# Routing tiles 20 to 25 one at a time instead of in pairs, in a fused involution and mixture-of-experts kernel

## The chip, the core and the metric

The kernel runs on one core of a Trainium2 chip. The metric is the device time of one execution in microseconds (us). PE is the matrix engine (TensorE), DVE the vector engine, ACT the scalar engine, POOL is GpSimd, and SP issues most of the plain DMAs. Each engine works through its own list of instructions in order; semaphores tie the lists together.

## What is computed

```python
# x: (4, 128, 56, 56) float32
def _L0_conv_ref(x, reduce_w, reduce_b, span_w, span_b):      # K=7, G=16 groups
    patches = conv_general_dilated_patches(x, (7, 7), ...)     # 49 shifted copies
    h = einsum('bchw,oc->bohw', x, reduce_w) + reduce_b        # 128 -> 32 channels
    kern = einsum('bchw,oc->bohw', h, span_w) + span_b         # 32 -> 49*16
    return (kern * patches).sum(axis=3)                        # a kernel per pixel
def _L0_ffn_ref(x, router_w, w1, w2, w3):                      # 8 experts, top 2, hidden 341
    probs = softmax(flat @ router_w.T)
    topk_probs, topk_idx = top_k(probs, 2)
    topk_probs = topk_probs / (sum(topk_probs) + 1e-09)
    h = silu(flat @ w1[e].T) * (flat @ w3[e].T)                # for every expert
    out = einsum('ne,nec->nc', gates, h @ w2[e].T)
x = x + _L0_conv_ref(_ln_c(x), ...)
t = _to_tokens(x)
t = t + _L0_ffn_ref(_ln_t(t), ...)
```

There are 4 x 56 x 56 = 12,544 tokens of 128 channels, and each goes to two of the eight experts.

## The kernel before

**Tiles and steps.** The image is cut into 28 tiles of 8 rows (448 tokens, handled as 4 groups of 112). All engines' lists are written out from one clock of steps `S`. Tile t has the steps 25t to 25t+24: in each step PE makes the per-pixel kernels of two taps (L635, into `kern_ps`), and DVE multiplies them with the shifted image (L901, or L895 with L898; the last, single tap is L889). The products are summed by POOL (L1144, L1148, into `acc_p`) and by PE (L650, into `acc_ps`). The convolution ends with step 699 (`CONV_END` = 700). DVE's L1106 adds the input and gives `x1` of tile t in step 5 of the next tile; then ACT computes the statistics, POOL takes the inverse root (L1134, L1136: `rsqrt`), ACT normalises (L807) and makes a second copy (the `twin`), PE transposes (L601) and computes the logits (L606).

**Routing.** Tiles are routed in groups (`GROUPS_OF`): the pairs (0,1) to (24,25), then 26 and 27 alone. One routing takes 41 DVE instructions: 19 of `route` (L924 to L970: the two best experts and their gates), 4 of `place` (L982 to L995: each row's place in the expert's list), 18 of `table` (L1013 to L1055: which blocks of 512 rows are full now). They are small, at most 128 elements a partition, and stand between DVE's products at fixed steps after `ROUTER_AT`, the start of the tile behind the group: `route` at offsets 19 to 31, `place` at 27 to 29, `table` at 33 to 41. ACT's two exponentials come at 24, its `gates` (L792) at 32, and PE's counting matmuls (`rank`, L611 and L614) at 26. For groups routed inside the convolution the scratch operands lie in PSUM, in spare columns of `kern_ps`; for the last ones they lie in SBUF (`small_sb`, `wide_sb`). For a pair of tiles the instructions work on 8 groups of 112 tokens at once, for a single tile on 4.

**Scatters.** Behind its routing each tile's rows go to memory (`xs`) with 8 indirect DMAs of POOL (L1157), at the steps of `SCATTER_J`; the first scatter of a tile waits for that tile's places and gates. Scatters that find no step before 700 are put behind the first blocks' adds by `BEHIND`.

**Blocks.** 56 blocks of 512 rows go through the experts, in the order in which groups complete them. A block is 6 slots on PE (3 matmuls each: L672, L673, L676), with ACT's silu (L832) and DVE's product (`hid`, L1074); then PE multiplies with w2 (`third`, L583, into the one PSUM `bank`), ACT scales by the gate (`y_tok`, L737), and POOL adds the rows to the output with 4 indirect DMAs (L1169). The first add of a block waits until all adds of the block before have landed. In the convolution slots are dealt out 11 in 25 steps, and 192 of the 336 slots stand there; behind it they follow each other. A block may be loaded when its group's table is there and all scatters up to that group have landed. `READY[g]` is the step from which the lists assume that. Blocks 40 to 55 need the last tile's group.

**Behind step 700** POOL's list reads: four adds of block 31 (step 704), four scatters, `rsqrt` of tile 27 (step 709), adds of block 32 (step 710), three scatters, and so on to block 37: 22 scatters, 6 of tile 25 and 8 each of tiles 26 and 27. From block 38 on there are only adds.

Of the kernel before, what the change touches and what calls it, by code (L numbers as in the profile page):

```python
# [23 lines left out]
TILES = B * PER_IMG  # L24
# [23 lines left out]

GROUPS_OF = [(2 * i, 2 * i + 1) for i in range(13)] + [(26,), (27,)]
NG = len(GROUPS_OF)
GMAX = max(len(g) for g in GROUPS_OF) * SUBS
BT = 512
BSUBS = BT // 128
NBLOCKS = (2 * TOKENS - EXPERTS) // BT + EXPERTS
FULL = [max(0, -(-(2 * N * (g[-1] + 1) - EXPERTS * (BT - 1)) // BT)) for g in GROUPS_OF[:-1]] + [NBLOCKS]

# [27 lines left out]
def at(p, j):  # L86
    return p * TAPS + j
# [22 lines left out]
def off(g, what):  # L110
    if g == NG - 1:
        return LAST_OFF[what]
    return {"route": ROUTE_OFF, "rank": RANK_OFF, "exp": EXP_OFF, "place": PLACE_OFF, "gates": GATES_OFF, "table": TABLE_OFF}[what]

ROUTER_AT = [at(tiles[-1] + 1, 0) for tiles in GROUPS_OF]
SCATTER_AT = {}
READY = []
_free = FIRST  # L120
for _g, _tiles in enumerate(GROUPS_OF):
    _S = max(_free, ROUTER_AT[_g] + off(_g, "place")[-1] + 1)
# [154 lines left out]
def build(nc, x, w_red, b_red, w_span, router, w13, w2, ident, lower, consts, tabs, ids, empty, out):  # L277
    with ExitStack() as ctx:
# [153 lines left out]
        def group_of(t):  # L432
            return next(i for i, tiles in enumerate(GROUPS_OF) if t in tiles)

# [811 lines left out]
```

## Time and profile before

| | us |
|---|---|
| median of 3 runs (lowest, highest) | 1472.53 (1470.37, 1472.7) |
| the profiled execution | 1467.69 |
| its span, first to last instruction | 1465.9 |
| busy in it: PE, DVE, POOL, ACT | 1247.6, 1119.5, 1082.7, 582.1 |

The profiled execution is 4.8 us shorter than the median and lies below all three timed runs. Inside the span the product of the last tap of the last tile (L889) ends at 1179.7 us; what follows, 286 us, is the stage in which the other 24 blocks are computed.

### The profile page before, as it was taken

What the parts mean: (1) busy time and instruction counts of PE and PEld (TensorE: products, weight loads), DVE (VectorE), ACT (ScalarE), POOL (GpSimd) and SP (SyncE); (2) the same over time, 40 slices, a digit from 0 to 9 for tenths busy, and PEclk for the clock granted to TensorE, in tenths of its full rate; (3) what the DMA queues carried; (4) which work ended last, traced back from release to release, by engine and by line L of the source; (5) the groups of instructions that cost most, each with busy time, mean ns of one, the idle gap of its engine ahead of it and who ended that gap; (6) DMA issues with size and microseconds to landing.
All of it is one profiled execution on the core that took longest, in us unless ns stands there. A gap on an engine that the chain in (4) does not pass through costs nothing.

```text
span 1465.9 us, 23321 instructions
## 1 busy us (share of the span) xinstructions
PE 1247.6 (85%) x7763; PEld 1027.1 (70%) x7763; DVE 1119.5 (76%) x1663; ACT 582.1 (40%) x1961; POOL 1082.7 (74%) x781
## 2 busy tenths in 40 slices
PE   5898998978988989899898998899989877788781
PEld 3677777767867777777777777777777766676561
DVE  7999999998898988888889798888898954232220
ACT  5334333333443434534345353354434343333230
POOL 4767787765785878787788687867878867856565
PEclk9999999998999999999999999999999988899996
DMA  4111111121242322433224232343322446666652
GB/s 127 61 42 54 57 58 52 58 79 55 39 106 59 86 63 61 101 69 86 60 61 104 65 92 57 62 100 83 73 54 53 108 102 181 129 162 146 140 118 24
DMA packets 93347, 120.42 MB, mean 82 GB/s; under 512 B 11531, under 2 KB 72428, under 8 KB 93082
## 3 DMA queue, kind: packets, MB, share of 16 engines
q1 hardware_dynamic: 53802, 90.97, 20.6%
q0 software_dynamic: 39424, 27.96, 13.8%
q8 instruction: 62, 1.02, 0.3%
q14 instruction: 59, 0.48, 0.1%
HBM read 78.92 MB, written 42.65 MB: 83 GB/s over the span
## 4 chain that ended last, share of the span: by engine, by line
PE 43%; DVE 27%; issue 12%; POOL 10%; DMA 5%; ACT 3%; DVEq 0%; SPq 0%; POOLq 0%; ACTq 0%
PE acc_ps L650 14%; PE kern_ps L635 13%; DVE prod L901 12%; PE bank L583 7%; POOL out L1169 7%; DVE kern_ps L895 4%; DMA out<-y_tok,idx 4%; PE h_ps L672 2%; PE h_ps L673 2%; PE h_ps L676 2%; DVE hid L1074 2%; DVE prod L898 2%; POOL acc_p L1148 1%; DVE kern_ps L1047 1%; DVE xf_lo L1099 1%
## 5 line engine op out<-in xcount | busy, mean ns | idle before, releaser
L901 DVE TENSOR_TENSOR prod<-kern_ps,xn 128x896 f32<-128x896 f32 x592 | 627.0, 1082 | 49.6 <-PE kern_ps L635 47.2
L635 PE MATMUL kern_ps<-h_stack,span 98*128 98x448 f32 x1372 | 465.8, 424 | 107.8 <-DVE prod L901 66.2
L1148 POOL TENSOR_TENSOR acc_p<-acc_p,prod 128x896 f32<-128x896 f32 x180 | 414.3, 2302 | 77.5 <-DVE prod L901 74.1
L1169 POOL DMA_INDIRECT out<-y_tok,idx x224 | 351.4, 1569 | 136.0 <-issue 60.0
L650 PE MATMUL acc_ps<-ident_sb,prod 128*112 128x128 f32 x2960 | 394.9, 277 | 0.0
L650 PEld LDWEIGHTS acc_ps<-ident_sb,prod 128*112 128x112 f32 x2960 | 347.2, 135 | 38.1 <-DVE x L1106 7.5
L635 PEld LDWEIGHTS kern_ps<-h_stack,span 98*128 98x128 f32 x1372 | 224.4, 198 | 198.0 <-DVE prod L901 113.2
L1157 POOL DMA_INDIRECT xs<-rows_x,slots x224 | 219.0, 978 | 53.4 <-issue 32.1
L583 PEld LDWEIGHTS bank<-w2b,hid 114*128 114x128 f32 x1344 | 182.8, 203 | 47.0 <-DVE xf_lo L1099 21.1
L583 PE MATMUL bank<-w2b,hid 114*128 114x128 f32 x1344 | 190.8, 289 | 23.8 <-DVE xf_lo L1099 12.1
L832 ACT ACTIVATE silu<-h_ps 114x512 f32<-114x512 f32 x132 | 78.9, 598 | 243.7 <-PE h_ps L676 243.7
L1074 DVE TENSOR_TENSOR hid<-silu,h_ps 114x512 f32<-114x512 f32 x132 | 90.0, 682 | 91.3 <-ACT silu L832 44.0
L1144 POOL TENSOR_TENSOR acc_p<-prod 128x896 f32<-128x896 f32 x28 | 63.8, 2279 | 89.3 <-DVE prod L901 52.2
L672 PE MATMUL h_ps<-xf_hi,wb 128*114 128x512 f32 x264 | 119.4, 452 | 7.4 <-ACT silu L832 7.4
L737 ACT ACTIVATE y_tok<-bank,xb 128x128 f32<-128x128 f32 x224 | 64.1, 371 | 127.7 <-PE bank L583 115.3
L676 PE MATMUL h_ps<-xf_lo,wb 128*114 128x512 f32 x264 | 107.5, 407 | 0.0
L673 PE MATMUL h_ps<-xf_hi,wb 128*114 128x512 f32 x264 | 107.5, 407 | 0.0
L895 DVE TENSOR_TENSOR kern_ps<-kern_ps,xn 128x896 f32<-128x896 f32 x80 | 87.2, 1090 | 12.7 <-PE kern_ps L635 11.8
L898 DVE TENSOR_TENSOR prod<-kern_ps,prod 128x896 f32<-128x896 f32 x80 | 87.3, 1091 | 2.7
L1074 DVE TENSOR_TENSOR hid<-silu,kern_ps 114x512 f32<-114x512 f32 x36 | 24.7, 687 | 72.4 <-ACT silu L832 40.5
L1134 POOL TENSOR_TENSOR rstd_ln<-veps_ln,minus_half 112x4 f32<-112x4 f32 x56 | 66.3, 1184 | 15.4 <-ACT veps_ln L770 15.3
L807 ACT ACTIVATE rows_x<-x,shift_ln,rstd_ln 112x128 f32<-112x128 f32 x112 | 47.8, 486 | 43.0 <-POOL shift_ln L1136 43.0
(157 smaller groups left out, 1342.4 us busy)
## 6 DMA issues: line engine op xcount, KB each, us to landing
wb<-wexp SPq DMA_DIRECT2D x56, 684.0 KB, 4.8
xb<-xs SPq DMA_DIRECT2D x56, 264.0 KB, 3.3
w2b<-in_w SPq DMA_DIRECT2D x56, 171.0 KB
xt<-in_x SPq DMA_DIRECT2D x28, 224.0 KB, 3.4
out<-x SPq DMA_DIRECT2D x28, 224.0 KB, 2.7
wexp<-wb SPq DMA_DIRECT2D x8, 684.0 KB
xs<-rows_x,slots POOLq DMA_INDIRECT x224, 2.4
out<-y_tok,idx POOLq DMA_INDIRECT x224
```

Source lines behind the costliest of these rows:

```text
L583: i = mm(bank[:, k * C:(k + 1) * C], hid[:, (CPE * b + c) % HR, k * 128:(k + 1) * 128], w2b[:, b % 2, c, :], start=c == 0 and k == 0, stop ...
L635: last = mm(kern_ps[:, g % 2, i, 0:N], span[:, k * C:(k + 1) * C], h_stack[:, t % 2, :], start=True, stop=True)
L650: last = mm(acc_ps[0:SUB, k * C:(k + 1) * C], src[:, at_:at_ + SUB], ident_sb[:], is_transpose=True, start=u == BY_PE[t][0] and i == 0 and ...
L672: mm(ps, lo, xf_hi[:, b % 2, :], start=True, stop=False)
L673: mm(ps, hi, xf_hi[:, b % 2, :], start=False, stop=False)
L676: mm(ps, hi, xf_lo[:, b % 2, :], start=False, stop=True).then_inc(done, 1)
L895: v.tensor_tensor(kern.rearrange("p i (r w) -> p i r w", w=W), kern.rearrange("p i (r w) -> p i r w", w=W), taps, ALU.mult).then_inc(s_inn ...
L901: v.tensor_tensor(pair_rows(dst), kern.rearrange("p i (r w) -> p i r w", w=W), taps, ALU.mult).then_inc(s_prod, 1)
L1074: v.tensor_tensor(hid[:, n % HR, :], silu[:, n % 2, :], h_at(n, 1), ALU.mult).then_inc(s_hid, 1)
L1148: g_.tensor_tensor(acc_p[:], acc_p[:], prod[:, (t * TAPS + u) % PRING, :], ALU.add).then_inc(s_padd, 1)
L1157: g_.indirect_dma_start(out=xs, out_offset=bass.IndirectOffsetOnAxis(ap=slots[:, k, n:n + 1], axis=0), in_=rows_x[:, t % XN2RING, q, k, :] ...
L1169: g_.indirect_dma_start(out=out, out_offset=bass.IndirectOffsetOnAxis(ap=idx[:, b % XBRING, q:q + 1], axis=0), in_=y_tok[:, b % 2, q * C:( ...
```

## The change

The list of groups is altered: tiles 20 to 25 are no longer taken as (20,21), (22,23), (24,25), each of the six is a group of its own. Everything else follows from the tables that are computed from this list.

```diff
-GROUPS_OF = [(2 * i, 2 * i + 1) for i in range(13)] + [(26,), (27,)]
+GROUPS_OF = [(2 * i, 2 * i + 1) for i in range(10)] + [(t,) for t in range(20, TILES)]
```

So there are 18 groups instead of 15. The six tiles have routings of 41 DVE instructions each, where three routings served them before. 194 slots instead of 192 stand in the convolution, and 16 scatters instead of 22 behind it. The last group, tile 27, keeps its steps (718 to 721).

On DVE, inside tile 22, from the addition of the input (L1106, `x`) to the next `hid` product, the list had only products of the convolution:

```order
L1106 TENSOR_TENSOR x<-acc_ps,xt 112x512
L901 TENSOR_TENSOR prod<-kern_ps,xn 128x896 x4
L1074 TENSOR_TENSOR hid<-silu,h_ps 114x512
L901 TENSOR_TENSOR prod<-kern_ps,xn 128x896 x2
L895 TENSOR_TENSOR kern_ps<-kern_ps,xn 128x2x448
L898 TENSOR_TENSOR prod<-kern_ps,prod 128x896
```

In the changed kernel the same place reads:

```order
L1106 TENSOR_TENSOR x<-acc_ps,xt 112x512
L901 TENSOR_TENSOR prod<-kern_ps,xn 128x896
L964 TENSOR_SCALAR kern_ps<-kern_ps 112x4
L966 RECIPROCAL kern_ps<-kern_ps 112x4
L968 COPY gid<-kern_ps 112x4
L970 TENSOR_TENSOR gid<-kern_ps,e 112x4
L901 TENSOR_TENSOR prod<-kern_ps,xn 128x896 x2
L1013 COPY kern_ps<-base 1x8
L1015 SCALAR_TENSOR_TENSOR full<-kern_ps,thr 1x200
L1018 TENSOR_REDUCE kern_ps<-full 1x8
L901 TENSOR_TENSOR prod<-kern_ps,xn 128x896
L1074 TENSOR_TENSOR hid<-silu,h_ps 114x512
```

The end of `route` and the whole `table` of tile 20 have come between tile 22's products; tiles 24 and 26 get those of tiles 22 and 24 in the same way.

On POOL, from the last scatters inside the convolution, the list before is:

```order
L1157 DMA xs<-rows_x,slots 104960x132 x2
L1169 DMA out<-y_tok,idx 13056x128 x4
L1157 DMA xs<-rows_x,slots 104960x132 x4
L1134 TENSOR_TENSOR rstd_ln<-veps_ln,minus_half 112x4
L1136 TENSOR_TENSOR shift_ln<-negmean_ln,rstd_ln 112x4
L1169 DMA out<-y_tok,idx 13056x128 x4
L1157 DMA xs<-rows_x,slots 104960x132 x3
```

And now:

```order
L1157 DMA xs<-rows_x,slots 104960x132 x2
L1169 DMA out<-y_tok,idx 13056x128 x4
L1157 DMA xs<-rows_x,slots 104960x132 x4
L1169 DMA out<-y_tok,idx 13056x128 x4
L1157 DMA xs<-rows_x,slots 104960x132 x3
L1134 TENSOR_TENSOR rstd_ln<-veps_ln,minus_half 112x4
L1136 TENSOR_TENSOR shift_ln<-negmean_ln,rstd_ln 112x4
L1169 DMA out<-y_tok,idx 13056x128 x4
```

Block 31's adds stand at step 700 instead of 704, block 32's at 708 instead of 710, and so block 32's adds with the three scatters behind them have passed in front of tile 27's inverse root, which stays at step 709. The four scatters behind block 31 were tile 25's; now they are tile 26's, whose places and gates are written for steps 704 and 707.

## Rows read from the trace of the kernel before

**Rows 1.** Windows of tiles 17, 18, 21, 22, 25, 26: us, busy PE PEld DVE ACT POOL, clock

```profile
681.81:731.38 49.57, 44.38 (x276) 37.01 (x275) 43.20 (x71) 19.84 (x69) 36.63 (x27) 0.93 0.36 81
731.38:774.26 42.88, 39.83 (x261) 33.31 (x260) 36.90 (x47) 20.02 (x69) 37.42 (x28) 1.00 0.28 55
...
864.32:911.64 47.32, 42.88 (x272) 36.74 (x271) 42.39 (x70) 23.05 (x80) 36.00 (x27) 0.93 0.36 84
911.64:955.90 44.26, 39.39 (x241) 32.73 (x240) 37.50 (x49) 15.47 (x52) 39.34 (x29) 0.96 0.28 56
...
1045.63:1094.04 48.41, 43.44 (x276) 35.67 (x275) 43.21 (x71) 19.85 (x69) 36.56 (x27) 0.96 0.35 78
1094.04:1136.05 42.01, 39.59 (x261) 33.31 (x260) 36.90 (x47) 19.89 (x68) 36.25 (x27) 1.00 0.27 51
```

**Rows 2.** DVE groups by form: shapes xcount | busy us, mean ns

```profile
L1018 DVE TENSOR_REDUCE kern_ps<-full 1x8 f32<-1x200 f32 x11 | 3.9, 357 | 0.4
L947 DVE TENSOR_TENSOR hit<-hit,kern_ps 112x64 f32<-112x64 f32 x13 | 2.9, 220 | 0.4
L1024 DVE TENSOR_REDUCE kern_ps<-cum 1x9 f32<-1x72 f32 x11 | 2.5, 224 | 0.4
L947 DVE TENSOR_TENSOR hit<-hit,small_sb 112x32 f32<-112x32 f32 x2 | 0.4, 192 | 0.1
```

**Rows 3.** One product of two SBUF operands (L1047): duration ns min/median/max, and forms

```profile
L1047 DVE TENSOR_TENSOR kern_ps<-ge,blk x11: 148/1699/2528, 274.4 to 1165.1; 1x3 f32<-1x3 f32 x6, 1x4 f32<-1x4 f32 x5
...
L1047 DVE TENSOR_TENSOR kern_ps<-ge,blk 1x4 f32<-1x4 f32 x5 | 9.4, 1879 | 0.0
...
L1047 DVE TENSOR_TENSOR kern_ps<-ge,blk 1x3 f32<-1x3 f32 x6 | 5.3, 878 | 0.5 <-PE kern_ps L635 0.5
```

**Rows 4.** Timeline (start us, us) of DVE's longest L1047 and POOL beside it

```profile
1076.59 2.53 DVE L1047 TENSOR_TENSOR kern_ps<-ge,blk 1x4 f32<-1x4 f32 x1
...
1076.43 2.65 POOL L1148 TENSOR_TENSOR acc_p<-acc_p,prod 128x896 f32<-128x896 f32 x1
```

**Rows 5.** Timeline of POOL behind the convolution, [idle before <-releaser]

```profile
1182.87 0.94 POOL L1157 DMA_INDIRECT xs<-rows_x,slots  x1 [0.30 <-issue]
1190.19 1.60 POOL L1169 DMA_INDIRECT out<-y_tok,idx  x1 [6.38 <-ACT y_tok L737]
...
1197.68 0.97 POOL L1157 DMA_INDIRECT xs<-rows_x,slots  x1 [0.30 <-issue]
...
1202.44 1.05 POOL L1134 TENSOR_TENSOR rstd_ln<-veps_ln,minus_half 112x4 f32<-112x4 f32 x1
1203.57 0.20 POOL L1136 TENSOR_TENSOR shift_ln<-negmean_ln,rstd_ln 112x4 f32<-112x4 f32 x1
...
1276.12 1.59 POOL L1169 DMA_INDIRECT out<-y_tok,idx  x1 [0.30 <-issue]
...
1289.01 1.54 POOL L1169 DMA_INDIRECT out<-y_tok,idx  x1 [5.75 <-DMA out<-y_tok,idx]
...
1321.07 1.54 POOL L1169 DMA_INDIRECT out<-y_tok,idx  x1 [4.75 <-ACT idx L732]
...
1452.15 1.54 POOL L1169 DMA_INDIRECT out<-y_tok,idx  x1 [2.42 <-DMA out<-y_tok,idx]
```

**Rows 6.** Timeline of the other engines there: PE, DVE, ACT

```profile
1179.07 0.61 DVE L889 TENSOR_TENSOR prod<-kern_ps,xn 128x448 f32<-128x448 f32 x1
...
1206.08 0.98 PE L601 MATMUL bank<-ident_sb,rows_x 112*128 112x112 f32 x4 [3.60 <-ACT rows_x L807]
...
1215.18 0.18 DVE L924 TENSOR_REDUCE small_sb<-lg 112x4 f32<-112x32 f32 x1
...
1219.98 0.22 DVE L995 TENSOR_REDUCE slots<-slot_h 112x8 uint32<-112x64 f32 x1
...
1194.77 0.20 ACT L792 ACTIVATE rows_x<-gid 112x16 f32<-112x16 f32 x1
...
1226.15 0.23 ACT L792 ACTIVATE rows_x<-gid 112x16 f32<-112x16 f32 x1
```

## The prediction

> **What bounds the kernel now.** I read three views, in this order. The first is the table of windows, one window a tile: a reader should see that the tiles come in two kinds. Tiles 17, 21 and 25 carry the end of a pair's route, its places and its table; tiles 18, 22 and 26 carry only the head of the next route. All six hold 11 slots of the experts. The first kind takes 49.57, 47.32 and 48.41 us (mean 48.4), the second 42.88, 44.26 and 42.01 us (mean 43.05), and DVE is busy for 42.9 against 37.1 us [rows 1]. So DVE works 86 to 89% of a tile, and the convolution grows nearly with its work. POOL does not: it is busy 36 to 39 us in both kinds. The second view is the timeline of POOL behind the convolution: once the adds of block 31 have begun it has little idle time, and from block 42 to block 55 it starts a new block's adds every (1452.15 - 1321.07) / 13 = 10.1 us [rows 5]. What counts there is when that chain starts and what stands in it besides adds. The third is the timeline of PE, DVE and ACT at tile 27's last normalisation and routing, which the adds are now moved across [rows 6].
>
> **Three more routings on DVE.** Executed back to back, the 23 instructions of route and place of a single tile take from 1215.18 to 1220.20 us, 5.0 us [rows 6]. A table has 18: two of 0.36 us, and sixteen between 0.15 and 0.22 us, which I count at 0.17; that is 3.4 us [rows 2, 3]. A single tile thus costs 8.4 us. A pair costs hardly more: the same product takes 220 ns on 64 elements and 192 ns on 32 [rows 2], so 23 x 0.028 = 0.6 us more, 9.0 us. A split turns 9.0 us into 16.8, which is 7.8 us more for each of three pairs.
>
> To this comes one instruction that is much longer than its work. L1047 multiplies 3 or 4 elements, both operands in SBUF, and takes from 148 to 2528 ns [rows 3]; the longest began 0.16 us behind a POOL sum of 2.65 us and ended with it [rows 4]. Over the 11 inside the convolution it is (9.4 + 5.3) / 11 - 0.15 = 1.2 us a routing [rows 3]. Each split adds one: 9.0 us, and 27 us for three.
>
> The Trainium skill (SBUF — State Buffer, Who interferes with whom) has a rule for this: a DVE instruction with two SBUF inputs and a GpSimd instruction that reads SBUF block each other, whoever comes second waiting for the whole of the other. The trace agrees with 2.53 us beside 2.65; by the rule each of the three new ones can wait for up to one POOL sum, so 0 to 7.5 us instead of 3.6.
>
> **How much of that the convolution pays.** From the second kind of tile to the first, DVE gets 13 - 10 more instructions of a pair's route and place (0.7 us), a table (3.4), the wait of L1047 (1.7 us in its form with four elements) and one more product for an expert block's input (estimated 0.7, as the other large ones): 6.5 us. The tile grows by 5.4 us [rows 1, 3]. That is 0.83 us a us; L1047 was above its mean in tile 25 [rows 4], so I take 0.8. The splits then cost 27 x 0.8 = 21.6 us, nearly all in tiles 22, 24 and 26, which become tiles of the first kind, the rest as route heads in 21, 23 and 25. The ends: 0.5 if the 6 us in which DVE is idle in such a tile take more of it (13.5 us), 1.0 if nothing hides it (27 us). ACT's three more pairs of exponentials and PE's counting matmuls I cost at nothing: ACT is busy under half of each tile, PE's work is halved with the tiles. POOL's six more scatters lie in tiles that get longer, with 5 us and more of POOL idle each; if that cover were gone they would cost 6 x 1.2 = 7.2 us, since four of them take 4.8 us [rows 5].
>
> The Trainium skill (VectorE: DVE Perf Modes, The TRN2 errata) gives a DVE instruction from PSUM to SBUF 120 cycles plus one an element at 0.96 GHz. That is 192 ns for 64 elements and 158 ns for 32, where the rows have 220 and 192. By the page a split would cost about 41 x 0.158 - 23 x 0.033 = 5.7 us instead of 7.8, and the three 16.6 us instead of 21.6. The rows decide.
>
> **Two slots more inside the convolution.** Tile 27 holds 11 slots instead of 9. A whole block of six takes 10.1 us in the steady chain [rows 5], so two are between 0 and 3.4 us; I take 1.5, the middle.
>
> **Behind the convolution,** in us from its end, 1179.68 [rows 6]. Before, POOL has its last scatter issued at +4.4 and waits until +10.5 for block 31's result [rows 5]. Now that result is written four steps earlier, ahead of step 700, and the adds start at +4.4. Four adds take 7.5 us [rows 5]: +11.9. This would be 6 us gained, but the list behind it has three new waits.
> First, the next scatter is now tile 26's and needs its gates. They were ready at +15.3 [rows 6], with block 31's w2 matmuls ahead of them, which are gone: I take +14. Four scatters take 4.8 us [rows 5], to +19, then block 32's adds to +26.5 and three scatters to +30.3.
> Second, only then comes tile 27's inverse root, ready at +31.6 where it was ready at +24.1 [rows 5]. It is 7.5 us late. PE already waited 3.6 us for it [rows 6], and everything behind PE's transposes waits with it. Its route began 11.4 us behind the inverse root [rows 5, 6], in which PE also did block 33's w2 work, now done before; I take 9.5, that is +41, places at +46. The gates came 11.0 us behind the route's start, since ACT was held by a block's result [rows 6]: between +46 and +52, I take +48.
> Third, tile 27's first scatter stands behind block 33's adds and waits for this. POOL gets there at about +43 and loses 5 us. Two scatters, block 34's adds, three scatters, block 35's adds and three scatters end at +73; before, the last scatter ended at +96.4 [rows 5].
> From there the chain has only adds. Block 36's start at +73, block 42's at 73 + 6 x 10.1 = +133.7. Before it was +141.4 [rows 5]. The tail gains 7.7 us: the early start and six scatters out of the chain, less two waits. Ends: 0, if the late routing eats it all, and 17.9, below.
>
> **The sum.** 21.6 + 1.5 - 7.7 = +15.4 us on the profiled execution of 1467.7, which gives 1483.1. That execution lies 4.8 us under the median of the three runs, so the median goes from 1472.5 to about 1488.
>
> **Rivals.**
> Rival 1, the tail wins (faster): the new routings fall into DVE's idle time and POOL never waits for routing. Half of 27 us less the tail's most: 6.1 us of early start, 6 x 1.2 = 7.2 for the scatters, and the uneven starts around block 40's late load, 1289.01 - 1276.12 - 10.1 = 2.8 us and 1321.07 - 1289.01 - 3 x 10.1 = 1.8 us [rows 5]: 17.9. Then 13.5 + 1.5 - 17.9 = -2.9 us, and 1470. It decides itself in tiles 22, 24 and 26: if they stay under about 46 us the change wins. For it: PE's granted clock was 1.00 in two of the second kind and 0.93 to 0.96 in the first, so a part of the 5.4 us may be the clock's and not DVE's. Against it: the first kind is long in all three cases.
> Rival 2, the tail gains nothing: the inverse root behind block 32's adds delays tile 27's routing so much that block 34 starts over 10 us late and the chain never catches up. Then 21.6 + 1.5 = +23, 1496. For it speaks that PE, ACT and DVE all wait in order for that one result. Against it: 16 scatters end well before the old 22.
> Rival 3, both the tiles and POOL are saturated: 27 + 1.5 + 7.2 - 7.7 = +28, 1500. For it: DVE has 6 us idle in a tile, and one new routing is 9 us. Against it: POOL's idle time in the same tiles.
> That the change does not do what it says is excluded: the order of instructions shows it.
>
> **Chances.** Forecast 0.63 (1480 to 1493), rival 1 0.10, rival 2 0.19, rival 3 0.08. Under 0.2% (3 us) a measurement of this kernel can't tell from no change. Rival 1 is spread over both sides of that: faster 0.07, same 0.05, slower 0.88. The range takes in rival 2 and most of the way to the others: 1476 to 1499.
>
> **What would show it.** Right: tiles 22, 24 and 26 take 47 to 49 us, L889 ends 20 to 26 us later, DVE busy grows by 22 to 27 us, L1047 appears three times more, POOL waits twice for ACT's gates (about 2 and 5 us), and the last scatter ends near +73. Wrong: even tiles under 45 us (the cost was overrated), or block 36's adds starting after +85 (the tail was). The forecast fails if DVE's work is not what sets the tile's length.

## The result, and the profile after

| | before | after |
|---|---|---|
| median, us (lowest, highest) of 4 runs each | 1471.45 (1470.22, 1472.7) | 1494.55 (1492.86, 1498.09) |
| ratio to before, 95% interval | | 1.0152 (1.013 to 1.0175) |
| the profiled execution, its span, us | 1467.69, 1465.9 | 1498.09, 1496.3 |
| end of the convolution (L889) | 1179.7 | 1193.2 |
| what follows, to the end of the span | 286.2 | 303.1 |

The change makes the kernel 23.1 us slower by the medians. The forecast was 1488 in a range of 1476 to 1499, with a chance of 0.88 for slower: the sign and the range held. Both terms behind the number did not, and they erred in opposite directions; that the time lies in the range is in part luck. The convolution was to cost 23.1 us, two slots included, and cost 13.6; the tail was to give back 7.7 us and cost 16.8 more. The two profiled executions are 30.4 us apart and the medians 23.1, so these terms, read from one pair of profiles, are together some 7 us too large; each is looked at below with runs of its own.

The first two lines of the page of the changed kernel, span and busy time of each engine:

```profile
span 1496.3 us, 23504 instructions
PE 1257.7 (84%) x7766; PEld 1033.5 (69%) x7766; DVE 1138.6 (76%) x1786; ACT 589.9 (39%) x1976; POOL 1082.7 (72%) x781
```

DVE is busy 19.1 us longer (1138.6 against 1119.5), POOL not at all. The windows of tiles 22, 24, 25 and 26 of the changed kernel, then of the stretches from the end of the convolution to the start of block 42's adds and from there to the end: start:end, us, busy PE, PEld, DVE, ACT, POOL (with counts), PE's granted clock, DMA share, GB/s:

```profile
913.12:960.03 46.91, 41.25 (x244) 33.99 (x243) 41.58 (x80) 16.37 (x54) 40.30 (x30) 0.93 0.28 54
1008.77:1052.60 43.83, 40.23 (x257) 32.84 (x256) 40.67 (x79) 20.24 (x70) 33.41 (x26) 1.00 0.29 68
1052.60:1102.42 49.82, 43.37 (x276) 36.07 (x275) 45.02 (x82) 22.96 (x74) 38.59 (x29) 0.97 0.32 73
1102.42:1148.05 45.63, 40.58 (x266) 33.41 (x265) 41.84 (x79) 20.47 (x71) 38.63 (x29) 1.00 0.36 80
1193.24:1348.68 155.44, 109.24 (x608) 89.28 (x607) 47.71 (x122) 53.79 (x141) 88.21 (x65) 0.85 0.57 131
1348.68:1496.30 147.62, 94.94 (x531) 73.22 (x529) 30.27 (x46) 38.59 (x106) 86.47 (x56) 0.87 0.52 102
```

Tiles 22 and 26 answer to [rows 1]: 44.26 and 42.01 us have become 46.91 and 45.63, at 41.6 and 41.8 us of DVE work instead of 37.5 and 36.9. DVE's counts show the change (80 instructions against 49). But tiles 24 and 26 did not become as long as tiles 17, 21 and 25 were before, 47 to 50 us, and tile 22 only just did not. Over tiles 21 to 27 together it is 328.1 us instead of 315.4.

The stalling product L1047 answers to [rows 3]: count, ns min/median/max, first and last start:

```profile
L1047 DVE TENSOR_TENSOR kern_ps<-ge,blk x14: 146/922/3172, 277.3 to 1176.5; 1x3 f32<-1x3 f32 x4, 1x4 f32<-1x4 f32 x4, 1x2 f32<-1x2 f32 x4, 1x1 f32<-1x1 f32 x2
```

There are three more, as forecast, but of the seven in tiles 21 to 27 five fall where POOL has no sum under way and take 0.15 us; the others take 2.34 (tile 21) and 3.17 (tile 25). Together they are 1.1 us longer than the four of before, and not 3.6.

Now the tail. The timeline of POOL after the convolution (start, us; in brackets the idle time before and what ended it). The rows are the last tiles' first gated scatter, tile 27's inverse root, block 33's adds, the scatter that needs tile 27's places, the last scatter, and block 36's adds:

```profile
1208.87 0.98 POOL L1157 DMA_INDIRECT xs<-rows_x,slots  x1 [4.50 <-issue]
...
1224.93 1.05 POOL L1134 TENSOR_TENSOR rstd_ln<-veps_ln,minus_half 112x4 f32<-112x4 f32 x1
...
1228.97 1.62 POOL L1169 DMA_INDIRECT out<-y_tok,idx  x1 [2.71 <-ACT y_tok L737]
...
1246.39 0.96 POOL L1157 DMA_INDIRECT xs<-rows_x,slots  x1 [8.95 <-DVE slots L995]
...
1270.49 0.94 POOL L1157 DMA_INDIRECT xs<-rows_x,slots  x1 [0.30 <-issue]
...
1281.42 1.59 POOL L1169 DMA_INDIRECT out<-y_tok,idx  x1 [9.99 <-ACT y_tok L737]
```

Counted from the convolution's end at 1193.24, the inverse root starts at +31.7 and is ready at +33.0 (forecast: ready at +31.6; before +24.1), the last scatter starts at +77.3 (forecast "near +73"; before about +95), and block 36's adds at +88.2 (forecast +73; before +73.9). Up to the last scatter the forecast is 4 us short. Then comes an idle stretch of 9.99 us that no part of it contains. POOL waits there for ACT's scaling of block 36's result. This is also the forecast's own sign of being wrong about the tail, block 36's adds after +85. PE, a step earlier, waits for the block's input:

```profile
1229.58 0.98 PE L601 MATMUL bank<-ident_sb,rows_x 112*128 112x112 f32 x4 [10.92 <-ACT rows_x L807]
...
1265.65 1.09 PE L620 MATMUL bank<-ident_sb,xb 128*128 128x128 f32 x4 [12.82 <-DMA xb<-xs]
```

The first row is the known wait for tile 27's root, 3.60 us before [rows 6] and 10.92 now. The second is new: 12.82 us for a DMA. The timeline of SP's queue in the changed kernel shows why it is late:

```profile
1250.95 10.22 SPq L514 DMA_DIRECT2D xs<-in_empty  x8
1262.22 1.53 SPq L533 DMA_DIRECT2D xb<-xs  x2
```

and the same queue in the kernel before, where the convolution ended at 1179.68:

```profile
1218.19 1.51 SPq L533 DMA_DIRECT2D xb<-xs  x2
...
1221.61 0.33 SPq L533 DMA_DIRECT2D xb<-xs  x1
...
1225.81 10.08 SPq L514 DMA_DIRECT2D xs<-in_empty  x8
```

The eight stores of `pad()` (L514, they fill the last blocks' unused rows) need the last tile's table and take 10 us to issue. Before, the loads of blocks 36 and 37 (L533) stood ahead of them on SP. In the changed kernel both loads have moved to step 722, and in step 722 `pad()` is written first. The loads are issued at +69, at the end of the stores, instead of at +38.5.

### The profile page after: what moved, and what is told of

It reads as the page before. It is cut to its first block, busy times and chain, and to the rows that moved or that the text cites. A ratio compares the mean times of both kernels' runs of the same rounds, so it can differ in the third digit from the quotient of the medians.

```text
span 1496.3 us, 23504 instructions
## 1 busy us (share of the span) xinstructions
PE 1257.7 (84%) x7766; PEld 1033.5 (69%) x7766; DVE 1138.6 (76%) x1786; ACT 589.9 (39%) x1976; POOL 1082.7 (72%) x781
## 3 DMA queue, kind: packets, MB, share of 16 engines
q0 software_dynamic: 39424, 27.96, 13.6%
## 4 chain that ended last, share of the span: by engine, by line
PE 40%; DVE 28%; issue 13%; POOL 10%; DMA 6%; ACT 3%; DVEq 0%; POOLq 0%; SPq 0%; ACTq 0%
PE acc_ps L650 14%; DVE prod L901 13%; PE kern_ps L635 12%; POOL out L1169 7%; PE bank L583 5%; DMA out<-y_tok,idx 5%; DVE kern_ps L895 4%; PE h_ps L672 2%; DVE hid L1074 2%; PE h_ps L673 2%; PE h_ps L676 2%; DVE prod L898 1%; POOL acc_p L1148 1%; DVE kern_ps L1047 1%; DVE xf_lo L1099 1%
## 5 line engine op out<-in xcount | busy, mean ns | idle before, releaser
L583 PE MATMUL bank<-w2b,hid 114*128 114x128 f32 x1344 | 190.4, 288 | 27.6 <-DVE xf_lo L1099 12.7
L672 PE MATMUL h_ps<-xf_hi,wb 128*114 128x512 f32 x266 | 121.7, 458 | 8.1 <-ACT silu L832 8.1
L673 PE MATMUL h_ps<-xf_hi,wb 128*114 128x512 f32 x266 | 109.0, 410 | 0.0
L895 DVE TENSOR_TENSOR kern_ps<-kern_ps,xn 128x896 f32<-128x896 f32 x80 | 87.1, 1089 | 13.4 <-PE kern_ps L635 12.7
L1099 DVE TENSOR_TENSOR xf_lo<-bank,xf_hi 128x512 fp32r<-128x512 f32 x56 | 38.5, 687 | 43.3 <-ACT xf_hi L729 43.2
```

Source lines behind the costliest of these rows:

```text
L583: i = mm(bank[:, k * C:(k + 1) * C], hid[:, (CPE * b + c) % HR, k * 128:(k + 1) * 128], w2b[:, b % 2, c, :], start=c == 0 and k == 0, stop ...
L672: mm(ps, lo, xf_hi[:, b % 2, :], start=True, stop=False)
L673: mm(ps, hi, xf_hi[:, b % 2, :], start=False, stop=False)
L895: v.tensor_tensor(kern.rearrange("p i (r w) -> p i r w", w=W), kern.rearrange("p i (r w) -> p i r w", w=W), taps, ALU.mult).then_inc(s_inn ...
```

## The experiments

Runs of different series are compared by their medians; where it matters, the text also compares each with the kernel before as it ran in the same series ("before of its own series"), since the median of before lay between 1469.9 and 1471.5 us.

The theory after this reading had three parts. The convolution pays about 13 us for three more routings, as DVE work. The late inverse root costs 8 to 15 us. The loads behind the stores cost about 10 us. The rival for the first part was something other than DVE's time (PE's counting matmuls, ACT's exponentials, the scatters in new places); the rival for the other two was that POOL, which has no long idle time in the steady chain, would lose the same time elsewhere. All kernels below keep the whole computation. "Tail" is the time from the end of the convolution to the start of the last block add in the profiled execution: 278.0 us before, 295.5 us after.

### The loads ahead of the stores

```diff
-                if S == ROUTER_AT[NG - 1] + off(NG - 1, "table")[-1] + 1:
-                    pad()
                 for what, b in LOAD_AT.get(S, []):
                     load_block(what, b)
+                if S == ROUTER_AT[NG - 1] + off(NG - 1, "table")[-1] + 1:
+                    pad()
```

> The changed kernel, with one thing altered on SP: at step 722 the loads of blocks 36 and 37 stand ahead of the eight pad stores, which wait for the last tile's table. Theory A (the pad stores in front of these loads hold the chain): PE no longer idles 12.8 us for block 36's rows, block 36's adds start about 9 us earlier than +88 us behind the convolution, and the time is 8 to 10 us under the changed kernel's 1494.6. Theory B (the tail is late only because tile 27's inverse root is late): PE's idle time moves, POOL's chain stays, and the time falls by under 3 us.

Measured: 1485.03 us (1.0098 of before, 1.0069 to 1.0128), 9.5 us less than the changed kernel; the tail is 282.1 us. SP's queue and POOL's start of block 36 in it:

```profile
1244.25 1.87 SPq L533 DMA_DIRECT2D xb<-xs  x2
...
1252.58 9.96 SPq L514 DMA_DIRECT2D xs<-in_empty  x8
```

Block 36's adds start at +79.2 with 0.34 us of idle time before them, against +88.2 with 9.99. The loads themselves are issued at +49.3 instead of +69.0: besides the 10 us of the stores' issue they no longer wait, with the stores, for the last tile's table. The queue's order alone was worth 9.5 us by the medians, and 8.0 us when each kernel is set against before of its own series (15.2 and 23.1 us above it).

### The inverse root ahead of block 32's adds

```diff
+ADD_AT[at(TILES, J_RSTD2) + 1] = ADD_AT.pop(at(TILES, J_RSTD2) - 1)
 SCATTERS_BEHIND = [4, 3, 3, 3, 3, 3, 4]
```

> The changed kernel, with one thing altered on POOL: block 32's adds and the three scatters behind them stand behind tile 27's inverse root (step 710 instead of 708), as in the kernel before. Theory A (late root and late loads each cost, one after the other): the root is ready 10 us earlier, the last routing too, POOL's wait of 9 us for tile 27's places goes, and the pad stores and block 36's load follow 8 us earlier: 8 to 10 us under the changed kernel. Theory B (the root alone is the cause): all of the tail's loss goes, 14 to 17 us under it.

Measured: 1480.67 us (1.0065, 1.0043 to 1.0087), 13.9 us less than the changed kernel (12.3 us against before of its own series); tail 276.4 us. The root is at +20.4 and the last scatter at +66.5, 10.8 us earlier. Block 36 still waits for ACT, 6.93 us, since its load still stands behind the stores. The expectation had 8 to 10 us for two separate losses and 14 to 17 for the root alone; the result lies between them. The loads are issued at +54.7 instead of +69.0, 14 us earlier where 8 were expected.

### Both together

The two edits above in one kernel, nothing else:

```diff
+ADD_AT[at(TILES, J_RSTD2) + 1] = ADD_AT.pop(at(TILES, J_RSTD2) - 1)
...
-                if S == ROUTER_AT[NG - 1] + off(NG - 1, "table")[-1] + 1:
-                    pad()
                 for what, b in LOAD_AT.get(S, []):
                     load_block(what, b)
+                if S == ROUTER_AT[NG - 1] + off(NG - 1, "table")[-1] + 1:
+                    pad()
```

> The changed kernel with both alterations. Theory A: both losses go; POOL's chain from block 31 to 36 is adds and scatters with one wait of 4 to 5 us for tile 26's gates; the tail takes 16 to 20 us less, 1475 to 1479, which is 3 to 8 us over the kernel before: what is left is the DVE work in the convolution less what the tail gains. If the two alterations only hide each other's loss, it is no better than the better of them alone, 1485.

Measured over 10 runs: 1473.12 us (1470.06 to 1479.81), 1.0023 of before (1.0005 to 1.0041), 21.4 us less than the changed kernel (19.9 us against before of its own series), and 2 us better than expected. POOL's timeline (the gated scatter, the root right behind its three fellows, block 36's adds):

```profile
1209.17 0.98 POOL L1158 DMA_INDIRECT xs<-rows_x,slots  x1 [4.50 <-issue]
...
1213.93 1.05 POOL L1135 TENSOR_TENSOR rstd_ln<-veps_ln,minus_half 112x4 f32<-112x4 f32 x1
...
1261.29 1.59 POOL L1170 DMA_INDIRECT out<-y_tok,idx  x1 [0.48 <-issue]
```

The tail is 268.3 us, 9.7 shorter than before. The rival falls: the time does not come back elsewhere. And tiles 21 to 27 take 328.2 us, as in the changed kernel: 12.8 more in the convolution, 9.7 less behind it, +3.1 in all, where the medians of before and of this kernel in one series differ by 3.2. This is the balance the change has without the late root and the late loads; the wait of 4.50 us for the gates is still in it.

### The late root alone, without the change

The kernel before, with block 32's adds moved from step 710 to 708, ahead of the inverse root:

```diff
+ADD_AT[at(TILES, J_RSTD2) - 1] = ADD_AT.pop(at(TILES, J_RSTD2) + 1)
```

> The kernel before, with one order altered on POOL: block 32's adds and the three scatters behind them stand at step 708, ahead of tile 27's inverse root, as the change has them. Nothing is added. The root should come about 11 us later. If the late root costs by itself, the time grows by 5 to 11 us, to 1475 to 1481. If it costs only beside the early result of block 31 or the late loads of block 36, it grows by under 3 us.

Measured: 1482.05 us, 1.0082 (1.0066 to 1.0098), 11 us slower than before, with no instruction of the convolution moved; the tail is 288.5 us, 10.5 us longer. Root on POOL, transposes on PE, and block 33's adds:

```profile
1213.84 1.05 POOL L1135 TENSOR_TENSOR rstd_ln<-veps_ln,minus_half 112x4 f32<-112x4 f32 x1
...
1217.47 0.98 PE L602 MATMUL bank<-ident_sb,rows_x 112*128 112x112 f32 x4 [14.88 <-ACT rows_x L808]
...
1225.17 1.63 POOL L1170 DMA_INDIRECT out<-y_tok,idx  x1 [10.01 <-ACT y_tok L738]
```

A root that comes 10 us later makes PE wait 14.88 us instead of 3.60 [rows 6], and POOL, which took the root late because it had adds to do, stands idle for 10 us when the same PE has not made the next block. The root is 10.3 us later (+33.1 instead of +22.8), PE is stopped 11.3 us longer and the run costs 11 us: the whole delay is paid, and this run doesn't tell the delay from PE's stop.

### Only DVE work, without the change

To tell DVE's time from everything else a routing brings, the kernel before got 123 reductions of 32 elements over 112 partitions, read from the identity matrix and used by nobody, in tiles 21 to 26 near the places where the changed kernel has its new routing instructions:

```diff
+EXTRA = {t: {0: 3, 2: 2, 4: 4, 6: 4, 8: 3, 10: 4, 12: 4, 14: 4, 16: 3} for t in (22, 24, 26)}
+EXTRA |= {t: {19: 3, 21: 4, 23: 3} for t in (21, 23, 25)}
...
                 routing(g)
+                extra(t, u)
```

> The kernel before, with 123 small DVE instructions more and nothing else: sums of 32 constants a partition, each waiting for the one before it, 31 in each of tiles 22, 24 and 26 and 10 in each of 21, 23 and 25, at the steps where the change puts its additional routing instructions. Each should take about 0.18 us, 22 us in all. The working of the prediction (0.8 us a us) expects the convolution to be 17 to 18 us longer and 1489; what the changed kernel's trace shows (12.8 us for 22.7 us of additional instructions) expects 11 to 13 us, 1483; if the changed kernel's longer tiles come from ACT or PE work of the three more routings, it stays under 5 us, 1476.

The group of these instructions (busy us, mean ns, idle before) and the windows of tiles 22, 24 and 26:

```profile
L887 DVE TENSOR_REDUCE idle_sum<-ident_sb 112x4 f32<-112x32 f32 x123 | 22.6, 184 | 6.1 <-PE kern_ps L639 3.0
```

```profile
912.09:960.52 48.43, 41.80 (x237) 34.10 (x235) 42.38 (x80) 15.34 (x52) 39.30 (x29) 0.90 0.27 53
1009.36:1053.44 44.08, 39.55 (x256) 32.66 (x255) 41.03 (x79) 19.60 (x69) 33.47 (x26) 1.00 0.26 61
1103.73:1149.31 45.58, 41.42 (x257) 34.18 (x256) 41.56 (x78) 19.77 (x68) 38.75 (x29) 0.96 0.26 49
```

Measured: 1484.2 us, 1.0095 (1.0069 to 1.012). Tiles 21 to 27 grow by 13.5 us for 22.6 us of DVE work, 0.6 us a us. The changed kernel's routing rows in these tiles add up to 22.7 us more than before and cost 12.8. So DVE's time alone is enough for the convolution's part, and the rival with PE, ACT and scatters is not needed. The rate over these tiles is 0.56 to 0.6 and not the 0.8 of the forecast; without tile 27, where the change also puts two slots more, it is 0.51 for the change (11.2 us for 22.1). It is an average of unequal tiles: 31 reductions, 5.7 us, cost 2.4 us in tile 24 and 4.2 and 3.6 us in tiles 22 and 26. PE's granted clock alone doesn't sort them: it is 0.90, 1.00 and 0.96 here, but in the changed kernel tile 26 stays at 1.00 and is 3.6 us longer all the same.

### Removing the stall of L1047, without the change

Where did the forecast's 0.8 come from? It compares tiles that hold a table with tiles that don't, and the table brings the long L1047. The timeline of the kernel before around that instruction in tile 25 (start, us, [idle before]):

```profile
1076.15 0.39 PE L673 MATMUL h_ps<-xf_hi,wb 128*114 128x512 f32 x1
...
1080.51 0.67 PE L635 MATMUL kern_ps<-h_stack,span 98*128 98x448 f32 x2 [2.63 <-DVE prod L901]
...
1083.99 0.63 PE L673 MATMUL h_ps<-xf_hi,wb 128*114 128x512 f32 x1
```

and windows of the same tile, just behind the stall and ahead of it:

```profile
1079.20:1083.00 3.80, 2.49 (x11) 2.18 (x12) 3.65 (x5) 0.00 (x0) 2.54 (x2) 0.78 0.15 22
1070.00:1076.60 6.60, 5.52 (x34) 4.19 (x33) 6.50 (x12) 2.33 (x6) 5.91 (x5) 1.00 0.61 163
```

DVE's 2.53 us stall [rows 4] leaves PE without a free `kern_ps` for 2.63 us. Its granted clock was 1.00 (2.4 GHz) up to the stall and is 0.78 over the 3.8 us from 1079.2, so for part of them it is at 1.2 GHz, and the same matmul that took 0.39 us takes 0.63. The experiment keeps the kernel before and only gives the product one operand in PSUM: a copy of `blk` into `past` one step earlier, an instruction with a single SBUF input.

```diff
                 elif k == 13:
+                    v.tensor_copy(past, blk[:, 2, 0:nb]).then_inc(s_past, 1)
...
-                    v.tensor_tensor(past, ge[:, 0:nb, EXPERTS], blk[:, 2, 0:nb], ALU.mult).then_inc(s_done, 1)
+                    dve.wait_ge(s_past, TABLES.index(g) + 1)
+                    v.tensor_tensor(past, ge[:, 0:nb, EXPERTS], past, ALU.mult).then_inc(s_done, 1)
```

> The kernel before, with one DVE copy more in each table (3 or 4 constants into PSUM, 0.15 us) and the long product L1047 reading one operand from there instead of both from SBUF. If it is the two SBUF operands that make it wait for a POOL sum, all its 11 cases in the convolution take 0.15 us, DVE has 13 us less; at 0.6 us a us the time falls by 6 to 8 us, to 1463 to 1465. If it waits for something else (its semaphore, the sums themselves), it keeps its mean of 1.3 us and the time stays.

Measured: **1447.83 us, 0.9833 of before (0.9819 to 0.9847)**, 23.3 us faster: three times what was expected, and the fastest kernel of this study. The product, the same place in tile 25, and the windows of tiles 18, 17, 21 and 25:

```profile
L1050 DVE TENSOR_TENSOR kern_ps<-ge,kern_ps x11: 140/142/154, 275.2 to 1142.2; 1x3 f32<-1x3 f32 x6, 1x4 f32<-1x4 f32 x5
```

```profile
1058.38 0.67 PE L636 MATMUL kern_ps<-h_stack,span 98*128 98x448 f32 x2 [0.23 <-DVE prod L902]
...
1061.03 0.40 PE L673 MATMUL h_ps<-xf_hi,wb 128*114 128x512 f32 x1
```

```profile
718.03:760.88 42.85, 39.80 (x261) 33.32 (x260) 36.91 (x47) 20.00 (x69) 37.41 (x28) 1.00 0.28 55
672.70:718.03 45.33, 41.78 (x276) 34.52 (x275) 40.79 (x71) 19.83 (x68) 36.65 (x27) 1.00 0.39 88
848.67:891.84 43.17, 40.26 (x272) 34.22 (x271) 40.09 (x71) 23.03 (x80) 36.01 (x27) 1.00 0.40 92
1025.82:1070.97 45.15, 41.95 (x276) 34.44 (x275) 40.73 (x72) 19.84 (x68) 36.65 (x27) 1.00 0.37 84
```

None of the 11 takes over 154 ns. Tiles 17, 21 and 25 are 4.2, 4.1 and 3.3 us shorter than in [rows 1], for stalls of 2.2 to 2.4 us each, and PE's clock in them is 1.00 instead of 0.93 to 0.96. The stalls summed to 9.4 + 5.3 - 11 x 0.15 = 13.0 us [rows 3]; without them tile 26 ends 23.0 us earlier (1113.03 instead of 1136.05). A stall of DVE here costs 1.4 to 1.9 times its length in these three tiles and some 1.8 times in all (from one profile of each kernel; at the end of tile 20 the profiles of kernels with this stall and the same tiles up to there lie between 862.2 and 867.7 us, with the PSUM operand at 848.7). In tile 25 PE stands idle for it, and then runs for a while at the lower level.

The convolution as a whole ends only 19.6 us earlier (1160.03), because a stall of the same kind has come up in tile 27. Tile 26's routing has its scratch operands in SBUF, and one of its products, 0.19 us in the kernel before, takes 3.48 us here; it ends with the POOL sum below. The group has two instructions, the other takes 0.19 us:

```profile
L948 DVE TENSOR_TENSOR hit<-hit,small_sb 112x32 f32<-112x32 f32 x2 | 3.7, 1834 | 0.1
```

```profile
1155.75 2.68 POOL L1151 TENSOR_TENSOR acc_p<-acc_p,prod 128x896 f32<-128x896 f32 x1
```

What is left between the first kind of tile and the second is 44.6 against 43.1 us, 1.5 of the 5.4 us. That is no rate of plain work. It is the mean of 2.5 us between tiles 17 and 18 and 3.1 between 25 and 26, all four at a clock of 1.00 and 3.9 and 3.8 us of DVE's busy time apart, and of -1.1 us between 21 and 22, where tile 22 has 0.96. Nor is every long tile one with a stall: tile 23, whose L1047 took 0.15 us before, takes 48.1 us in both kernels.

The Trainium skill (SBUF — State Buffer, Who interferes with whom) has the rule used here: DVE and GpSimd share one port pair of SBUF under an exclusive lock, which a DVE instruction with two SBUF inputs needs. The trace agrees: 2.53 us beside POOL's 2.65 us sum with both operands in SBUF, 0.14 us beside a POOL sum when one is in PSUM. In the changed kernel the case of 3.17 us began 0.51 us ahead of POOL's sum and ended with it, so a DVE row that starts first can wait as well.

### Is the gates' wait on the path?

The mended kernel, with the four scatters behind block 31 put after later blocks:

```diff
-SCATTERS_BEHIND = [4, 3, 3, 3, 3, 3, 4]
+SCATTERS_BEHIND = [0, 4, 4, 4, 4]
```

> The changed kernel with both alterations (loads ahead of the pad stores, root ahead of block 32's adds) and none of the 16 scatters behind block 31: four each behind blocks 32 to 35, so that POOL meets tile 26's first scatter a block later, when its gates are long ready. If the wait of 4.5 us for the gates is paid by the chain, the time falls by 3 to 5 us under the kernel with both alterations (1473.1), to about 1469, the kernel before. If POOL is not what ends the chain there, it is the same within 2 us.

Measured: 1475.44 us over 12 runs (1.0034, 1.0013 to 1.0055), against 1.0023 with the wait in place. The expectation missed. POOL's 4.5 us are gone, but it then waits for the statistics of tile 27 (6.57 us ahead of the root, which comes only 2.7 us earlier), and block 36 stands at +71.9 instead of +67.7. The chain as a whole doesn't pay for the wait in this order. That the wait costs nothing by itself isn't shown, since four scatters now stand behind each of four blocks.

### Fewer splits

One split (only tiles 24 and 25 alone), two splits, and one split with the stores put behind the loads of step 724 too:

```diff
-GROUPS_OF = [(2 * i, 2 * i + 1) for i in range(10)] + [(t,) for t in range(20, TILES)]
+GROUPS_OF = [(2 * i, 2 * i + 1) for i in range(12)] + [(t,) for t in range(24, TILES)]
```

The first has the loop order of the first experiment; in the second (`range(11)`, singles from 22) the root is moved as well; the third is the first with `pad()` three steps later:

```diff
-                if S == ROUTER_AT[NG - 1] + off(NG - 1, "table")[-1] + 1:
+                if S == ROUTER_AT[NG - 1] + off(NG - 1, "table")[-1] + 4:
                     pad()
```

> Only the pair (24,25) is split; the loads of blocks 36 and 37 stand ahead of the pad stores, and the root is ahead of block 32's adds by the table itself. 20 scatters stand behind the convolution instead of 22, and block 31's adds begin where they did. A third of the additional DVE work should cost the convolution about 4 us (3.6 in tile 26, little in 25). The tail has hardly anything to gain: two scatters less, 2 us at most. So 1472 to 1475, 2 to 4 us over the kernel before. If the cost is not the DVE work but something at the convolution's end, it stays as with three splits.

> The pairs (22,23) and (24,25) are split, with both alterations. Block 31's result comes as early as with three splits, 18 scatters stand behind. By the account of work and tail the convolution costs 8 to 9 us instead of 13, and the tail gains 8 to 10: 1468 to 1472, equal to the kernel before or a little under it, and 1 to 4 us under the kernel with three splits and both alterations. If the convolution's cost is not proportional to the splits it is the same as that one.

> The kernel with only the pair (24,25) split, with the pad stores at step 725, really behind the loads of blocks 36 and 37. In the run before, these loads stood at step 724, behind the pad stores of step 722, and block 36's adds began 17.9 us behind block 35's instead of 11.3. If the pad stores were the cause, that distance is 11 to 12 us and the time falls by 4 to 6 us under 1472.5, to 1466 to 1469, under the kernel before. If it was something else (the first matmuls of blocks 36 and 37, which both wait for the rows), it stays within 2 us of 1472.5.

| | median us (runs) | ratio to before | end of the convolution | tail |
|---|---|---|---|---|
| one split | 1472.45 (12) | 1.0021 (1.0009 to 1.0033) | 1182.4 | 279.3 |
| two splits | 1474.08 (9) | 1.0021 (1.0005 to 1.0037) | 1194.7 | 271.4 |
| one split, stores last | 1469.53 (12) | 0.9987 (0.9975 to 1.0000) | 1183.5 | 274.6 |

In the first, the loads of blocks 36 and 37 stand at step 724 and `pad()` at 722, so the swap inside a step did not help; POOL's start of block 36:

```profile
1257.63 1.59 POOL L1169 DMA_INDIRECT out<-y_tok,idx  x1 [6.99 <-ACT y_tok L737]
```

With the stores last that wait falls to 2.3 us and the kernel is 2.9 us faster by the medians, the second sighting of this queue, less than the 4 to 6 us expected. It ties with before. Two splits were expected at 1468 to 1472 and missed it. No number of splits gives a clear gain: what a split brings to the tail it takes from the convolution. Two splits were no cheaper in the convolution than three in the one profile of each, because tiles 26 and 27 took 48.3 and 48.6 us there. In tile 27 two products of two SBUF operands stall, of the kind seen above (1.74 and 3.31 us, shortest 0.19); in tile 26 none does. The window of tile 26 with two splits, then mended with three:

```profile
1097.80:1146.12 48.32, 43.67 (x266) 36.03 (x265) 42.14 (x79) 20.47 (x71) 38.64 (x29) 0.93 0.35 75
```

```profile
1102.67:1148.35 45.68, 40.59 (x266) 33.42 (x265) 41.85 (x80) 20.45 (x71) 38.65 (x29) 1.00 0.36 80
```

The busy times of the engines agree within 0.3 us apart from PE, which has the same 266 matmuls at a clock of 0.93 instead of 1.00.

### The splits without the stall

The PSUM operand, its edit as above, in the kernel with one split and the stores last, and in the one with three splits and both waits mended:

> Both at once: one split with the pad stores last, and the PSUM operand. If both are right and add up, 3 us for the split's tail and 7 for the operand, 1460 to 1463, the fastest of all. If the gains meet on the same path, the better of the two alone.

> The changed kernel with both alterations of the tail, and with L1047 reading one operand from PSUM. Against the same kernel without the PSUM operand (1473.1) the long waits of L1047 in the convolution go. Measured so far: three splits cost the convolution 12.7 us, the mended tail gives back 9.7, the PSUM operand alone is worth 23 us. If these add up: 1447.8 + 3 = 1451. If the routings' cost was mainly the waits of L1047, the splits now cost the convolution under 8 us and it is at or under 1448, the fastest. One split with the PSUM operand gave 1453, which speaks for the first.

Measured: 1453.09 us (0.9878, 0.9859 to 0.9897) and 1458.06 us (0.9906, 0.9875 to 0.9937; six runs from 1450.29 to 1465.8). Both are behind the 1447.83 of pairs with the PSUM operand, and both missed their expectations: 1460 to 1463 and "the fastest of all" for one split, and 1451, or 1448 and less, for three. Three splits cost some 10 us on this base, where they cost 3 us on the old one. In the profile of the second, its slowest run, the tail is 273.3 us, shorter than the 278.4 of pairs, so the loss is in the convolution: tiles 21 to 27 take 329.4 us, against 311.4 for pairs with the PSUM operand and 328.2 for three splits without it. Tiles 21 and 25 are 3.9 and 3.6 us shorter than in the latter, without their stalls, and tiles 22, 26 and 27 are 2.6 to 3.3 us longer. Part of tile 27 is a stall again:

```profile
1177.85 3.30 DVE L949 TENSOR_TENSOR hit<-hit,small_sb 112x32 f32<-112x32 f32 x1
```

and tiles 26 and 27 show a lower clock:

```profile
1086.00:1183.00 97.00, 86.00 (x530) 72.20 (x529) 88.22 (x161) 36.13 (x118) 78.77 (x58) 0.93 0.34 76
```

Why the clock is lower in tile 26 in this kernel and in the one with two splits, and not with three splits and the stall of L1047 (0.98 over the 91.5 us of its tiles 26 and 27), is open. No experiment of this study separates it, and none gives the products of tile 26's routing a PSUM operand.

## Why the prediction was right, step by step

The sign and the range were right; of what the forecast named as signs of being right, the three more L1047 and the two waits of POOL came, the second of them for tile 27's places and not its gates. Tiles 22, 24 and 26 at 47 to 49 us, the convolution 20 to 26 us longer and DVE busy 22 to 27 us more did not.

**Work of a routing: nearly right.** The forecast put 7.8 us of DVE rows on each split, 23.4 us on three without stalls and 27 with them. The rows of tiles 21 to 27 grow by 22.7, of which 1.9 us are stalls (1.1 in L1047, 0.8 in L932 of tile 27). A single tile's routing is 7.6 us instead of 8.4. The 192 ns of [rows 2] belong to a product with both operands in SBUF; with one in PSUM, as in these routings, it takes 187 ns. DVE's busy time grew by 19.1 us against 22 to 27.

**The stall of L1047: the term was over-sized.** 1.2 us a routing was the mean of the 11 before; the new places mostly miss POOL's sums. 1.1 us came instead of 3.6. The sign of the price was right for the wrong reason: what these stalls cost was not 0.8 of their length but 1.8 times.

**The rate: the step that failed in the convolution.** The forecast divided 5.4 us by 6.5 and took 0.8. The two kinds of tile differ in a stall as well as in work, and it was priced at 1.7 of the 6.5 us; without it the same tiles differ by 1.5 us, so it had carried 3.9 of the 5.4. The rate for plain work is 0.51 to 0.6 over these tiles, by the change and by reductions that do nothing. The forecast's 21.6 us was about 9 us too much: some 3 for work and stalls that did not come (22.7 instead of 27), the rest for the rate. How far 0.5 to 0.6 carries is open: single tiles range from 0.4 to 0.7, and three splits on the kernel without the stall cost 18 us in tiles 21 to 27 of its one profile. It had the warning in hand, in its first rival: PE's clock of 0.93 to 0.96 in the first kind. This was read as a possible part of the 5.4 us, and the rival was given 0.10.

**Two slots more: within its bounds, not shown by itself.** Tile 27 takes 1.6 us more (forecast 1.5), but 0.8 us of that is the longer stall of L932, and where another product stalls in it, in the runs with the PSUM operand and with the late root alone, the same tile takes 47.0 us without the two slots.

**The tail up to the last scatter: order right, sizes short.** Block 31's adds start at +4.0 (forecast +4.4), the root is ready at +33.0 (+31.6). The two named waits came in their places, at 4.5 us (2.1) and 8.95 us (5), and the last scatter stands 4 us late. Moving the root alone shows this step's price on the whole run: 13.9 us in the changed kernel, 11 us when added to the kernel before; the forecast had 5 us of POOL's waiting for it.

**Behind it: a queue was left out.** "From there the chain has only adds" assumed that block 36's rows were there. The loads' move from step 718 and 721 to 722, behind stores of 10 us on SP, is in none of its terms. Its price is 8.0 to 9.5 us. With both orders mended the tail gains 9.7 us, near the 7.7 that the forecast gave it, but that agreement proves little: the 7.7 has the late root's 5 us of waiting in it, which this kernel doesn't have, so the forecast's own terms would give it about 12.7. What failed is the list of what the moved steps pass.

**The sum.** By the profiles +13.6 and +16.8 instead of +23.1 and -7.7: errors of -9.5 and +24.5 us that partly cancel. The first lies at the lower end of what the forecast allowed for that term (13.5 and no slots), the second outside its ends (a gain of 0 to 17.9). By the medians the change costs 23.1 us instead of 15.4, and the time is 6.6 us above the forecast. Rival 2 (1496, the tail gains nothing because the late root holds up everything) had the right mechanism for half of the tail and came nearest in time, with a convolution that was too dear. Rival 1's test, tiles 22, 24 and 26 under 46 us, was nearly met (46.9, 43.8, 45.6), and the change did not win: the test looked only at the convolution.

## What to carry to other kernels

When work moves on a clock of steps, list for every queue what now stands in front of what, the queue that issues plain DMAs included: a batch of small stores ahead of a load cost over six tenths of what three routings did in the convolution (8.0 to 9.5 us against 12.8). A rate read from two kinds of stretches is a rate of all in which they differ; take out the stalls first, or put in work that does nothing and measure. And a short instruction that at times takes seventeen times its shortest is worth removing before anything is rearranged: here one operand in PSUM brought 23 us, and no split brought anything.

## What the runs showed of the hardware that was not expected

- A stall costs more than its length. 13.0 us of DVE stalls in the convolution were worth 23.0 us by the end of tile 26: behind the one of 2.53 us PE is idle for 2.63 us, its granted clock, 1.00 before, is 0.78 over the 3.8 us from 1079.2, and single matmuls go from 0.39 to 0.63 us.
- It is not one instruction's property. Products of two SBUF operands elsewhere, in tile 26's routing, take 0.93 us (before), 1.70 (the change), 3.48 (pairs with the PSUM operand) instead of 0.19. Which of them stalls changes from kernel to kernel.
- Small DVE instructions added to tiles in which DVE is busy for 85% and more cost 0.6 of their time over six tiles (22.6 us for 13.5), and between 0.4 and 0.7 in single ones. PE's granted clock alone doesn't say which: tile 26 paid 3.6 us at 0.96 and, in the changed kernel, at 1.00.
- The eight stores of SP take 9.7 to 10.3 us to issue in twelve of the profiles, 1.3 us each, and in the changed kernel the loads that stand behind them are issued only after the last.
- The same tile 26, with the same instructions on every engine, takes 48.32 us in one kernel and 45.68 in another, and PE's granted clock, 0.93 against 1.00, is what differs in its window. What sets it there stayed open.
